# Row scatters paced by sets of value matmuls, expert tiles ten rounds later, gathers two to a set

## The reference, cut to what matters

```
xn = layernorm(x)
q, k, v = xn @ Wq, xn @ Wk, xn @ Wv        # per head, times cos(phase) * amplitude
w = softmax(q @ k.T / sqrt(8) * cos(2 pi (i - j) / S))
attn = ((w + roll(w, 1)) / sqrt(2)) @ v @ Wo
logits = from xn @ wqkv.T                  # 8 a token
for the two best experts e of a token:
    h = xn @ w1[e].T;  a, g = split(h)
    ffn += score_e * (silu(a) * g @ w2[e].T)
out = x + attn + ffn
```

## Time and profile before

| | |
|---|---|
| median of 3 runs | 688.54 us |
| the 3 runs | 687.61, 688.54, 947.86 us |
| profiled execution, span | 724.2 us |
| PE, ACT, DVE, POOL busy in it | 616.4, 526.8, 257.0, 82.3 us |

### The profile page before, as it was taken

The page is one execution under the profiler, slowest core; times in us unless marked ns, Lnnn a source line. Parts: engine busy times, 40 slices in busy tenths (PEclk is TensorE's granted clock), DMA queues, the critical chain, the costliest instruction groups (busy, mean ns, idle before and its releaser), DMA issues.

```text
span 724.2 us, 11825 instructions
## 1 busy us (share of the span) xinstructions
PE 616.4 (85%) x4317; PEld 221.3 (31%) x4317; DVE 257.0 (35%) x587; ACT 526.8 (73%) x489; POOL 82.3 (11%) x95
## 2 busy tenths in 40 slices
PE   3868661499999999999999999999899999888885
PEld 1322110133333333333333333334333333212213
DVE  6662700244124334342434334343424343000042
ACT  2658930278887878777786878778787877999992
POOL 4100077300000000000000000000000000445300
PEclk9978955599999999999999999999999999999999
DMA  8335921002441321212222122223132200111002
GB/s 244 110 118 175 247 77 53 14 1 79 169 138 39 101 85 58 93 62 87 69 82 76 60 89 71 85 72 110 38 111 71 79 8 12 28 30 37 25 1 62
DMA packets 49581, 57.33 MB, mean 79 GB/s; under 512 B 7356, under 2 KB 39126, under 8 KB 49266
## 3 DMA queue, kind: packets, MB, share of 16 engines
q1 hardware_dynamic: 46384, 52.04, 22.7%
q0 software_dynamic: 2048, 4.20, 1.9%
q10 hardware_dynamic: 1090, 0.30, 0.2%
HBM read 21.14 MB, written 13.63 MB: 48 GB/s over the span
## 4 chain that ended last, share of the span: by engine, by line
PE 61%; ACT 13%; issue 12%; DVE 6%; another core or an unknown queue 4%; DMA 1%; ACTq 1%; SPq 0%; DVEq 0%
PE ps L1309 25%; PE ps L1292 12%; ACT big L665 11%; PE ps L1228 7%; PE ps L1237 5%; PE ps L1326 4%; DVE m L984 4%; PE ps L1112 1%; PE ps L1316 1%; PE ps L1179 1%; ACT cs L657 1%; ACTq L591 1%; PE ps L1218 1%; PE ps L1267 1%
## 5 line engine op out<-in xcount | busy, mean ns | idle before, releaser
L665 ACT ACTIVATE big<-ps 128x1536 f32<-128x1536 f32 (+1 forms) x410 | 483.2, 1244 | 149.9 <-PE ps L1292 120.9
L1309 PE MATMUL ps<-big,vh 128*32 128x512 f32 x2048 | 268.5, 614 | 0.0
L1292 PE MATMUL ps<-qa,ka 49*128 49x512 f16 x896 | 161.0, 390 | 54.3 <-ACT big L665 27.6
L984 DVE TENSOR_REDUCE m<-ps 128x1 f32<-128x512 f32 x128 | 88.5, 692 | 125.7 <-PE ps L1326 125.7
L1292 PEld LDWEIGHTS ps<-qa,ka 49*128 49x128 f16 x896 | 38.7, 94 | 208.9 <-ACT big L665 154.3
L1228 PE MATMUL ps<-xgT,store 128*128 128x128 f32 (+1 forms) x468 | 72.5, 292 | 0.0
L1309 PEld LDWEIGHTS ps<-big,vh 128*32 128x32 f32 x2048 | 45.8, 110 | 71.7 <-issue 56.6
L1228 PEld LDWEIGHTS ps<-xgT,store 128*128 128x128 f32 (+1 forms) x468 | 55.8, 182 | 25.5 <-issue 25.5
L546 POOL COPY vh<-vaug 128x144 f32 x16 | 5.1, 320 | 503.8 <-PE ps L1309 481.1
L1326 PE MATMUL ps<-ka,attnT 49*128 49x512 f16 x128 | 48.5, 379 | 15.3 <-DVE m L984 15.2
L931 DVE SCALAR_TENSOR_TENSOR cs<-cs,ps 128x384 f32<-128x384 f32 x39 | 21.6, 555 | 59.2 <-ACT cs L657 59.2
(11 more groups left out here) (172 smaller groups left out, 270.3 us busy)
## 6 DMA issues: line engine op xcount, KB each, us to landing
store<-w1T SPq DMA_DIRECT2D x39, 352.0 KB, 2.5
store<-w2T SPq DMA_DIRECT2D x39, 192.0 KB, 2.6
qk_parts<-store SPq DMA_DIRECT2D x16, 256.0 KB
qa<-qk_parts SPq DMA_DIRECT2D x27, 128.0 KB
slots_x<-vh SPq DMA_DIRECT2D x5, 512.0 KB, 6.5
cs<-slots_x SPq DMA_DIRECT2D x20, 128.0 KB, 2.5
slots_y<-y SPq DMA_DIRECT2D x19, 128.0 KB, 2.4
store<-in_L_ffn_w SPq DMA_DIRECT2D x4, 512.0 KB, 6.5
```

What stands on the lines that cost most here:

```text
L665: nc.scalar.activation(probs[:, prob_of(tiles[0]):prob_of(tiles[-1]) + 1, :], ps[:, bank_of(tiles[0]):bank_of(tiles[-1]) + 1, :], ACT.Exp, ...
L984: nc.vector.tensor_reduce(m4[:, NT * r + i, c:c + 1], ps[:, O_BANKS[(p - 1) % 2], :], AX, ALU.max).then_inc(m_reduced, 1)
L1292: ins = nc.tensor.matmul(ps[:, bank_of(n), :], k[at:at + KQ, P * o:P * o + P], q[at:at + KQ, CW * c:CW * c + CW], start=True, stop=True, t ...
L1309: ins = nc.tensor.matmul(ps[32 * c:32 * c + 32, O_BANKS[p % 2], :], vh[:, p % 2, o + 8 * b, :], probs[:, prob_of(n), :], start=k == 0, sto ...
```

## The change

The numbers in the order tables are the lines of each kernel (those of the changed kernel are two or four higher). The scatters no longer stand in two blocks: for w from 14 to 45, one is issued once w sets of value matmuls are done, and the clearing of `attnT` follows the last. The expert tiles begin in round 39 in place of 29, and with them the DMAs that go by `EXPERTS_AT`; SP's first two loads of rows and the staging of the first three experts' weights stand in round 37 (in place of 28), the weights ahead of the rows. The gathers begin at 224 sets in place of 209, two to a set.

```diff
-EXPERTS_AT = 29
+EXPERTS_AT = 39
+SCATTER_AT = 14
-GATHER_AT = 209
+GATHER_AT = 224
+GATHERS_A_QUAD = 2
...
-                if r == WEIGHTS_AT + E * NF // 2:
+                if r == EXPERTS_AT - 2:
+                    for first in range(STAGES - 1):
+                        stage_weights(first)
                     load_rows(0)
                     load_rows(1)
-                    for first in range(STAGES - 1):
-                        stage_weights(first)
...
-            for r in range(2):
-                for t in range(NT):
-                    nc.gpsimd.indirect_dma_start(slots_x, ..., xn[:, t, :], None).then_inc(scattered, 16)
-                if r == 0:
-                    pool.wait_ge(pv_done, QUADS)
-                    head_values(2)
-
-            pool.wait_ge(scattered, 2 * NT * 16)
-            nc.gpsimd.memset(qe[:], 0.0).then_inc(rows_ready, 1)
-
-            for w in range(2 * QUADS, H * QUADS):
-                if w % QUADS == 0 and w // QUADS + 1 < H:
+            for w in range(SCATTER_AT, H * QUADS):
+                if w >= QUADS and w % QUADS == 0 and w // QUADS + 1 < H:
                     pool.wait_ge(pv_done, w)
                     head_values(w // QUADS + 1)
-                j = w - GATHER_AT
+                i = w - SCATTER_AT
+                if i < 2 * NT:
+                    pool.wait_ge(pv_done, w)
+                    scatter_rows(i)
+                if i == 2 * NT:
+                    pool.wait_ge(scattered, 2 * NT * 16)
+                    nc.gpsimd.memset(qe[:], 0.0).then_inc(rows_ready, 1)
+                j = GATHERS_A_QUAD * (w - GATHER_AT)
...
                 if 0 <= j < 2 * NT:
                     pool.wait_ge(pv_done, w)
-                    gather_result(j)
+                    for k in range(GATHERS_A_QUAD):
+                        gather_result(j + k)
```

More of the change, by code:

```diff
@@ L561, in _, with scatter_rows @@
             pool.wait_ge(slot_ready, 1)
-            for r in range(2):
-                for t in range(NT):
-                    nc.gpsimd.indirect_dma_start(slots_x, bass.IndirectOffsetOnAxis(ap=slot[:, r, t:t + 1], axis=0),
-                                                 xn[:, t, :], None).then_inc(scattered, 16)
-                if r == 0:
-                    pool.wait_ge(pv_done, QUADS)
-                    head_values(2)
-            pool.wait_ge(scattered, 2 * NT * 16)
-            nc.gpsimd.memset(qe[:], 0.0).then_inc(rows_ready, 1)
-            for w in range(2 * QUADS, H * QUADS):
-                if w % QUADS == 0 and w // QUADS + 1 < H:
+            def scatter_rows(j):
+                r, t = j // NT, j % NT
+                nc.gpsimd.indirect_dma_start(slots_x, bass.IndirectOffsetOnAxis(ap=slot[:, r, t:t + 1], axis=0),
+                                             xn[:, t, :], None).then_inc(scattered, 16)
+            for w in range(SCATTER_AT, H * QUADS):
+                if w >= QUADS and w % QUADS == 0 and w // QUADS + 1 < H:
                     pool.wait_ge(pv_done, w)
                     head_values(w // QUADS + 1)
-                j = w - GATHER_AT
+                i = w - SCATTER_AT
[6 more added lines that the diff above has]
+                j = GATHERS_A_QUAD * (w - GATHER_AT)
                 if j == 0:
```

## The result

The changed kernel takes 698.92 us (median of 4 runs, 697.73 to 699.87), the kernel before 690.72 us beside it (median of 4). The ratio, which leaves the run of 947.86 us out, is 1.0119, with a 95% interval of 1.008 to 1.0158: slower by about 1.2%, and within the 2% that was forecast as "same". The profiled execution of the changed kernel took 699.19 us for a span of 697.2, so 2.0 us lie around the span.

The account below looks back on a forecast made before the run. It took PE to be busy nearly everywhere, except a profiled hole in rounds 12 to 15 beside POOL's scatters, absent from timed runs. Terms: 688.5 + 0 + 0 + 3 = 691.5, rounded to 691 us; 8-in-10 range 681 to 702.

Parts of the forecast that it names:

- What the change takes out of the profile it cannot take out of the median.: Rounds 12 to 15: the profiled execution has the 34.1 us hole in PE's work, the two low timed runs do not.
- Scatters: POOL's scatters paced by sets: 34.1 us out of the profile, 0 (from -5 to 0) in timed runs.
- scatters 2.4 to 2.9 us apart: Sign expected in the changed kernel's profile: the spacing of POOL's paced scatters.
- Experts ten rounds later: Expert tiles moved: ten rounds lose them, rounds 167 to 176 gain them, 5.1 us each way; sum 0, within 1 us.
- The loads for the last two heads: SP's 16 loads, behind head 4's, land 3.5 us late for the first job on PE: +3 us (0 to 4).
- is not what ends last: Clearing of `attnT`, around round 39: over within 1 us of that round's start, while SP is still with head 4.
- Gathers: From 224 sets, two to a set: DVE waits 3.7 us at the additions, covered with 10 us to spare: 0.
- Rival 2: Back-to-back gathers from 649 us hold up PE's signals, costing 34 us, so 725; chance 0.09 in median, 0.35 in profile.
- Rival 1: The hole of rounds 12 to 15 is in timed runs too, so they gain 34.1 us: 657; chance 0.10.
- Rival 3: The hole comes from clock or chain of rounds 12 to 15 and stays: timed 691, profiled span 727; chance 0.10.
- Sum: Whole timed run: 688.5 + 0 + 0 + 3 = 691.5, rounded to 691 us; range 681 to 702.

Follow-up runs that it names:

- before_again: The kernel before, unchanged, timed against itself: 692.99 us, ratio 1.0009.
- experts_only: Changed kernel with scatters back to back and the 16 loads for the last two heads in round 29 again: 743.6 us, ratio 1.0212 to the kernel before.
- late_loads: Kernel before with only SP's 16 loads for the last two heads moved from round 29 to 39: 733.07 us, ratio 1.0091.
- exact_first: Changed kernel with SP's 16 loads for the last two heads ahead of head 4's loads: 696.88 us, ratio 1.006 to the kernel before.
- gathers_only: Kernel before with the gathers alone changed, from 224 sets, two to a set: 692.0 us, ratio 1.000.
- two_a_set: Changed kernel with scatters two to a set and the 16 loads in round 33: 716.7 us, ratio 0.9859 to the kernel before.
- after_again: The changed kernel, unchanged, timed again in another job: 712.01 us against 722.82 for the kernel before.

## Why the prediction was right, and where not

- **"What the change takes out of the profile it cannot take out of the median."** Right for the runs it spoke of, and shown: before_again has the dense scatters, no hole, and 2.0 us around its span, so that 688.5 us leaves no room for a hole of 34. The inference was too wide in one word: I took the stall for chance of single executions. In three jobs of four every run of the kernel before is longer, by 27 us at the least (719.04 against 692.07) and by 31 to 34 in the median. That the result was measured in a free job, like the two low runs shown, was luck: the 712.01 us of the same kernel in a held-up job lie outside the range of 681 to 702. The 947.86 us remain unexplained; no trace of such a run was seen.
- **Scatters: 0 in a timed run, 34.1 in a held-up one.** Both hold in the main: 27.87 against 27.67 us for sets 13 to 23 in free conditions, 33.2 to 36.9 us gained in held-up ones (31.5 to 35.6 were the bounds). One sign named there held only in part: scatters 2.4 to 2.9 us apart. In rounds with two sets two of them go out 1.27 us apart, and the mean is 2.27.
- **Experts ten rounds later: 0.** Right: -0.2 us over the stages in experts_only. The two rates of the earlier trace rows were read rightly.
- **The loads for the last two heads: +3 us (0 to 4).** The mechanism and the place were right, and the wait of 3.80 us is within the bounds. The term was mis-sized: it measured 6.0. What the working left out is the clock. It stood at half speed for 6.8 us, the first 1.1 of them within PE's idle stretch; the 6 us from 186 on saw 21 matmuls, 6 us at full speed 40. A half clock beside a hole stood in the earlier trace rows and should have been priced: in these traces a PE wait of a few us costs six to eight tenths as much again behind it. The 3.80 us became 6.0 in the stage; in late_loads the wait of 2.71 us became 4.8 in the stage and 6.7 in the median; in exact_first 2.08 became 3.35.
- **The clearing "is not what ends last".** True for the changed kernel, where it was over at 173.0 and the 16 loads began at 177.02, but by so little that exact_first ran into it at once.
- **Gathers: 0.** Right in free conditions, gathers_only 1.000, with DVE's 10 us to spare measured at 9.10.
- **Rival 2, the gathers take the scatters' place.** Right in kind, wrong in price: 14.8 us for 32 gathers (0.46 each), not 34. (14.7 in experts_only and 15.4 in two_a_set.) It does not touch the median of the result; in after_again it does, beside the gain at the scatters.
- **Rival 1, the hole is in the timed runs too.** False where the result was measured, true in three other jobs, though with 712 us and not 657: there the kernel before starts from 723 and not from 688. Rival 3, that pacing leaves the hole, is out by after_again.
- **Sum.** 691 was forecast, 698.92 measured, within the 681 to 702. Of the 7.9 us, 3 are the loads' term. The rest is mostly the base: 688.54 was the median of the three runs shown, while 30 runs of the free job gave 692.07, and the times of the kernel before have steps of 1 to 2 us that go with its mean granted clock. Against 692.07, of another job, the changed kernel is 6.9 us slower, and its span is 5.4 us longer than that of gathers_only; the 6.0 of the loads lie between the two. That 691 is in the range does not make the sum good: it missed by more than twice the one cost that it named.

The Trainium skill (SBUF — State Buffer, "SBUF: two separate sides") has PE never wait on another user of the buffer. In the free job the trace agrees: scatters 1.28 us apart, PE busy for 10.82 of 13.41 us beside them. In held-up jobs it does not agree as a rule for the kernel: DVE and ACT sat waiting for PE's signals for 8 to 26 us at a time while POOL issued (the earlier trace rows and late_loads). Whether the held-up path is one to SBUF, or that of the signals themselves, no run here tells.

**What stays open:** what differs between the jobs (the chip, where buffers lie in DRAM, or something else). The chip bears the number 0 in the free job and in the first held-up one (1 and 11 in the others), so if that is the same chip, the chip alone does not decide. Also open are why a gather costs less than half of a scatter, and the path on which PE is held up. Late fetching of instructions is not what the traces show: the instruction queue q8 moves its next packet right after set 20 both in the first trace (at 148 us, behind the hole) and in before_again (at 112 us), so none is seen to be late.

## What to carry to other kernels

When the span of a profile and the timed runs disagree by the length of one stall, do not choose one of them: run the unchanged kernel again, in more than one job, and price the change for both conditions. Moving a wait's producer (here the scatters, then the clearing, then 16 loads) costs what the last consumer's slack allows, and where the consumer is PE, count the half-speed stretch that comes with the wait as well as the wait. Issue indirect DMAs from POOL one at a time, each behind a wait on PE's progress, at both ends of a kernel: one to a set (2.3 us apart on the mean for the scatters, 1.95 for the gathers) cost nothing here in either condition, and the density that was harmless in one job cost 33 us in another.

## What the runs showed of the hardware that I had not expected

- In three of four jobs (traced in two, by its times alone in the last), scatters issued back to back (1.28 us apart) held up PE and its signals by 1.0 to 1.2 us each; in the two of them that had gathers back to back, these cost 0.46 to 0.48 us each. At one to a set (2.25 us apart on the mean) scatters cost nothing that the stages show (26.34 against 26.07 us for sets 13 to 23); at 2.01, 1.74 and 1.55 us on the mean some 7, 9 and 10 us were lost over the 32.
- The hold-up does not go with the bytes: 64 scatters of 64 KB, and 32 of 64 KB with 32 of 16 KB between them, gave the same (73.7 and 75.9 us).
- With PE waits of 3.80, 2.71 and 2.08 us the granted clock stood at the 1.2 GHz level for 6.8, 6.8 and 3.4 us, from 1.1 us before the end of the first wait, from the end of the second, and from 2.2 us after the end of the third.
- The spans of one unchanged kernel fall into steps (685.5 to 692 us) that match the mean granted clock of the run, 0.987 to 0.972.
